# Layer 3 of a DLRM tower with samples on partitions: swapping the two operands of its matrix product

## The chip, the core and the metric

The kernel runs on one core of one Trainium2 chip. Its engines are TensorE (PE in the profile; its weight loads have a row of their own, PEld), VectorE (DVE), ScalarE (ACT), GpSimd (POOL) and SyncE (SP). Each has its own instruction stream, and they meet at semaphores. The metric is the device time of one execution in microseconds; the median of several executions counts.

## What is computed

For 2048 samples, 27 embedding tables give one row of 128 numbers each. All 351 pairs of these 27 rows are multiplied (dot products), joined with a dense feature vector of 128, and sent through three layers of 512, 256 and 1 outputs.

```python
e = jnp.stack([tbl_0[ids[:, 0]], ..., tbl_26[ids[:, 26]]], axis=1)      # 2048 x 27 x 128
interactions = jnp.einsum('bfd,bgd->bfg', e, e)                         # pairs
x = interactions.reshape(B, F * F)[:, TRIL_IDX]                         # 351 of them
z = jnp.concatenate([r_bottom_mlp_out, x], axis=1)
h = jnp.concatenate([z, r_bottom_mlp_out], axis=1)                      # 607
h = jnp.maximum(h @ W_top1 + b_top1, 0.0)                               # 512
h = jnp.maximum(h @ W_top2 + b_top2, 0.0)                               # 256
y = h @ W_top3                                                          # 1: the layer of the change
```

## The kernel before

The batch is worked in 8 half blocks of 256 samples (HALF), each of two tiles of 128 (TILE). In every half block:

- features: 11 tables of 1000 rows are read by one-hot products (onehot_unit, line 728): VectorE makes the one-hot tiles (line 433), TensorE multiplies them by the table. The other 16 tables are gathered by GpSimd (line 393) and transposed by TensorE (transpose_tile, line 740). ScalarE copies both into embT (lines 541 and 548).
- products of pairs: pair_products (line 754) for tile 0 and tile 1, in the last half block end_products (line 766). VectorE and ScalarE copy the products to SBUF (lines 446 and 559), SyncE writes them to DRAM (write_gram, line 315) and reads them back rearranged (read_pairs, line 325); ScalarE and VectorE split what was read (lines 573 and 408).
- dense layers, one half block late: while half block i has its features and products made, the layers of half block i - 1 run between them. On TensorE, second_rows(i, dense) puts them in this order: layer 1 (line 774) and layer 2 (line 802) around the transpose of tile 1's third bank, then the transpose of its fourth bank, then layer 3 (line 810), and then the products of tile 1.
- On ScalarE the order is the same: layer 2's two results (line 584), the embT copy of the fourth bank (line 548), then layer 3's copy to y (line 597), then the products' copies.
- SyncE stores y (line 295) at the end of its half; behind it stand the next ids' load (line 281) and the four gram stores of tile 1.

The order of the work is written out by hand in each engine's stream; half block 1 stands by itself, 2 to 6 are a loop (Fori) and 7 stands by itself again. In half block 7 all eight PSUM banks serve the dense layers, and its layers run alone at the end.

Layer 3 before: the weights w3 (one column for each of two chunks of 128 hidden units) are the stationary operand, and layer 2's result h2 (128 hidden units x 256 samples) streams. The result is one row of 256 on one partition. The samples of a tile stand in the order "k j" (k of 4, j of 32), where sample j * 4 + k is meant, so ScalarE's copy to y also reorders, and the store is one contiguous row of 1 KB.

Of the kernel before, what the change touches and what calls it, by code (L numbers as in the profile page):

```python
# [7 lines left out]
HALF, TILE = 256, 128  # L8
HALVES = BATCH // HALF
FIRST, LAST = 0, HALVES - 1  # L10
PAD = 32
GROUP = 4
# [10 lines left out]
def is_half(i, h):  # L23

    return isinstance(i, int) and i == h
# [31 lines left out]
def dlrm_tower(nc, bottom, ids, ids_onehot, tables, w_bottom_a, w_pairs, w_bottom_b, b1, w2, b2, w3, scratch, out):  # L57
    fp32, fp32r, i32 = mybir.dt.float32, mybir.dt.float32r, mybir.dt.int32
# [50 lines left out]
    JT = TILE // GROUP  # L109
# [9 lines left out]
    M1, M2 = H1 // 128, H2 // 128  # L119
# [20 lines left out]
    with ctx:  # L140
        def sb(name, shape, dt):
            return ctx.enter_context(nc.sbuf_tensor(name, shape, dt))
# [6 lines left out]
        KIB = 1024  # L149
# [6 lines left out]
        def in_arena(name, shape, dt, at):  # L156
            return nc.alloc_sbuf_tensor_at(name, shape, dt, offset=arena_at + at)
# [7 lines left out]
        packed = in_arena("packed", [J, GROUP, PAIRS], fp32, 13 * KIB // 2)  # L165
        pairX = in_arena("pairX", [CHUNK, 3, HALF], fp32, 13 * KIB)
        h2 = in_arena("h2", [128, M2, HALF], fp32, 16 * KIB)
        y = in_arena("y", [1, HALF], fp32, 18 * KIB)
        w1p_raw = in_weight_arena("w1p_raw", [CHUNK, 3, H1], fp32, 0)
        w1b_raw = in_weight_arena("w1b_raw", [128, H1], fp32, 6 * KIB)  # L170
        w1b_more = in_weight_arena("w1b_more", [128, H1], fp32, 12 * KIB)
# [19 lines left out]
        w3s = sb("w3s", [128, M2], fp32)  # L191
# [36 lines left out]
        dense_act = sem("dense_act")  # L228
# [4 lines left out]
        out_done = sem("out_done")  # L233
        WEIGHT_LOADS = 7
        TILE_OUT = 16 * GROUP


        def gram_piece(t, b):
# [15 lines left out]
        def dense_at(i, w):  # L254

            ring = all_banks if is_half(i, LAST) else ps_dense
            return ring[w % len(ring)]
# [12 lines left out]
        def _(sp):  # L270
# [21 lines left out]
            def store(i, at):  # L292
                sp.wait_ge(dense_act, (M2 + 1) * (i + 1))
                sp.sem_inc(loads_begun, 1)
                sp.dma_start(out[bass.ds(at, HALF), :].rearrange("b o -> o b"), y[:, :]).then_inc(out_done, 16)

            def next_ids(i, m, at, n):

# [18 lines left out]
            def read_pairs(i, some):  # L317

                if 0 in some:
                    sp.wait_ge(gram_out, TILE_OUT * 2 * (i + 1))  # L320
                    sp.sem_inc(loads_begun, 1)
# [50 lines left out]
                half(i, sp.snap(i * HALF))  # L372
            half(LAST, LAST * HALF, False)
            store(LAST, LAST * HALF)
            sp.wait_ge(out_done, 16 * HALVES)

        @block.gpsimd
        def _(pool):
# [27 lines left out]
        def _(dve):  # L406
# [30 lines left out]
            def empty_gram(i, t):  # L437
                if t == 0 and not is_half(i, FIRST):
                    dve.wait_ge(gram_out, TILE_OUT * 2 * i)
                if is_half(i, LAST):  # L440
# [71 lines left out]
        def _(act):  # L512
# [74 lines left out]
            def layer3(i):  # L587
                w = use_y(i)
                act.wait_ge(densed, DENSE * i + w + 1)
                if not is_half(i, FIRST):  # L590
                    act.wait_ge(out_done, 16 * i)
                bank = dense_at(i, w)[0:1, 0:HALF]
                if is_half(i, LAST):
                    nc.scalar.copy(y[:, :].rearrange("p (j k) -> p k j", k=GROUP),
                                   bank.rearrange("p (k j) -> p k j", k=GROUP)).then_inc(dense_act, 1)
                else:
                    nc.scalar.copy(y[:, :].rearrange("p (t j k) -> p t k j", t=2, k=GROUP),
                                   bank.rearrange("p (t k j) -> p t k j", t=2, k=GROUP)).then_inc(dense_act, 1)

            def features(i, dense=None):  # L600

# [66 lines left out]
            for u in range(1, RG, 2):  # L668
                act.wait_ge(densed, DENSE * LAST + u + 1)
                for dst, src in pack_pieces(u):  # L670
                    last = nc.scalar.copy(dst, src)
# [10 lines left out]
        def _(pe):  # L682
# [123 lines left out]
            def layer3(i):  # L806
                bank = dense_bank(i, use_y(i))
                for c in range(M2):
                    pe.wait_ge(dense_act, (M2 + 1) * i + c + 1)
                    last = nc.tensor.matmul(bank[0:1, 0:HALF], w3s[:, c:c + 1], h2[:, c, :],  # L810
                                            start=(c == 0), stop=(c == M2 - 1))
                last.then_inc(densed, 1)

            def relayout():
# [127 lines left out]
```

## Time and profile before

| | us |
|---|---|
| median of 3 runs | 408.24 |
| lowest and highest | 406.95 and 410.33 |
| span of the profiled execution | 600.9 |
| TensorE busy, matmul | 416.6 |
| TensorE busy, weight load | 378.3 |
| GpSimd busy | 253.9 |
| VectorE busy | 198.2 |
| ScalarE busy | 143.3 |

The profiled execution is a different one from the three timed ones, and its own time beside them is its span, 600.9 us. Times of rows below are microseconds from its start. A matmul with fp32 operands appears as two records, each with its own weight load. "Idle before" is the time in which the engine did nothing ahead of a group, with what ended it; "issue" means that nothing in the profile ended it. Layer 3 of the seven half blocks 0 to 6 appears once in each of seven turns, at 175.7, 246.2, 316.0, 384.9, 454.4, 524.6 and 574.9 us.

### The profile page before, as it was taken

What the parts mean: (1) busy time and instruction counts of PE and PEld (TensorE: products, weight loads), DVE (VectorE), ACT (ScalarE), POOL (GpSimd) and SP (SyncE); (2) the same over time, 40 slices, a digit from 0 to 9 for tenths busy, and PEclk for the clock granted to TensorE, in tenths of its full rate; (3) what the DMA queues carried; (4) which work ended last, traced back from release to release, by engine and by line L of the source; (5) the groups of instructions that cost most, each with busy time, mean ns of one, the idle gap of its engine ahead of it and who ended that gap; (6) DMA issues with size and microseconds to landing.
All of it is one profiled execution on the core that took longest, in us unless ns stands there. A gap on an engine that the chain in (4) does not pass through costs nothing.

```text
span 600.9 us, 11581 instructions
## 1 busy us (share of the span) xinstructions
PE 416.6 (69%) x4550; PEld 378.3 (63%) x4550; DVE 198.2 (33%) x523; ACT 143.3 (24%) x256; POOL 253.9 (42%) x263
## 2 busy tenths in 40 slices
PE   0444655786498836897298955899378972979888
PEld 0434644676388836697186944788276962979766
DVE  3405612265204612074013722065022730138111
ACT  2302321124031221224022230322122230312423
POOL 6773563256440671526622563406723365220000
PEclk9975887698597976999579985989578995889989
DMA  7964721236112461144312461124311362122000
GB/s 161 236 146 108 191 60 52 59 76 107 36 50 54 94 104 42 36 81 92 84 36 53 88 108 31 52 59 93 96 41 31 95 92 70 41 59 52 11 2 1
DMA packets 50590, 44.79 MB, mean 75 GB/s; under 512 B 30211, under 2 KB 43019, under 8 KB 50562
## 3 DMA queue, kind: packets, MB, share of 16 engines
q1 hardware_dynamic: 40746, 25.82, 22.2%
q0 software_dynamic: 8192, 16.79, 10.8%
q10 hardware_dynamic: 1623, 1.79, 1.2%
q8 instruction: 19, 0.31, 0.2%
q14 instruction: 10, 0.07, 0.0%
HBM read 39.52 MB, written 4.85 MB: 74 GB/s over the span
## 4 chain that ended last, share of the span: by engine, by line
PE 63%; issue 23%; another core or an unknown queue 5%; DVE 4%; ACT 2%; DMA 1%; SPq 1%; ACTq 0%; DVEq 0%
PE ps_build L728 26%; PE ps_gram L754 16%; PE ps_dense L774 8%; PE ps_dense L802 4%; PE ps_build L740 3%; DVE hot L433 2%; PE ps_gram L740 2%; DMA raw<-tbl_dram 1%; PE ps_dense L810 1%; PE ps_gram L774 1%; DVE table L408 1%; ACT embT L541 1%; PE ps_gram L766 1%; PE ps_gram L821 1%
## 5 line engine op out<-in xcount | busy, mean ns | idle before, releaser
L393 POOL DMA_INDIRECT rows<-tbl_dram,idx x256 | 253.1, 989 | 275.6 <-PE ps_gram L740 96.2
L728 PE MATMUL ps_build<-hot,table 125*128 125x256 f32 x1408 | 196.3, 299 | 60.1 <-DVE table L408 34.0
L728 PEld LDWEIGHTS ps_build<-hot,table 125*128 125x128 f32 x1408 | 184.9, 204 | 65.6 <-issue 53.8
L754 PE MATMUL ps_gram<-embT 128*53 128x52 f32 x1792 | 99.5, 254 | 107.2 <-issue 106.5
L754 PEld LDWEIGHTS ps_gram<-embT 128*53 128x53 f32 x1792 | 80.8, 166 | 127.9 <-issue 125.4
L433 DVE TENSOR_SCALAR hot<-id_raw 125x512 fp32r<-125x512 f32 (+1 forms) x384 | 133.8, 408 | 76.4 <-remote 33.3
L446 DVE COPY gram<-ps_gram 117x416 f32<-117x416 f32 x28 | 16.6, 592 | 229.8 <-remote 151.1
L541 ACT COPY embT<-ps_build 128x512 f32<-128x512 f32 (+1 forms) x48 | 37.7, 786 | 176.9 <-PE ps_build L728 82.8
L559 ACT COPY gram<-ps_gram 117x416 f32<-117x416 f32 x28 | 14.2, 506 | 178.7 <-PE ps_gram L754 130.1
L774 PE MATMUL ps_dense<-pairT,w1p 120*128 120x256 f32 (+1 forms) x252 | 37.1, 295 | 0.0
L774 PEld LDWEIGHTS ps_dense<-pairT,w1p 120*128 120x128 f32 (+1 forms) x252 | 34.9, 206 | 0.0
L740 PE MATMUL ps_build<-ident,rows 128*128 128x128 f32 x128 | 20.4, 286 | 8.8 <-issue 6.9
L802 PE MATMUL ps_dense<-h,w2s 128*128 128x256 f32 x112 | 25.3, 379 | 0.0
L423 DVE TENSOR_SCALAR id_raw<-id_raw,vocab 125x512 f32<-125x512 int32 (+1 forms) x48 | 22.2, 462 | 6.2 <-DMA id_raw<-ids_onehot_dram 6.2
L548 ACT COPY embT<-ps_build 128x512 f32<-128x512 f32 x32 | 21.4, 669 | 7.4 <-PE ps_build L740 4.9
L548 ACT COPY embT<-ps_gram 128x512 f32<-128x512 f32 x32 | 21.6, 675 | 4.2 <-DVE w1b L408 2.2
L740 PEld LDWEIGHTS ps_build<-ident,rows 128*128 128x128 f32 x128 | 15.4, 146 | 11.4 <-issue 10.6
L802 PEld LDWEIGHTS ps_dense<-h,w2s 128*128 128x128 f32 x112 | 20.8, 190 | 2.6
L579 ACT ACTIVATE h<-ps_dense,b1s 128x256 f32<-128x256 f32 x28 | 13.3, 473 | 30.6 <-PE ps_dense L774 30.6
L408 DVE TENSOR_TENSOR pairT<-pairX,pairT 120x256 fp32r<-120x256 f32 (+1 forms) x21 | 7.7, 421 | 36.0 <-issue 18.9
L740 PE MATMUL ps_gram<-ident,rows 128*128 128x128 f32 x128 | 19.3, 272 | 0.0
L774 PE MATMUL ps_dense<-botT,w1b 128*128 128x256 f32 x84 | 17.6, 323 | 0.0
(57 smaller groups left out, 147.6 us busy)
## 6 DMA issues: line engine op xcount, KB each, us to landing
id_raw<-ids_onehot_dram SPq DMA_DIRECT2D x40, 256.0 KB
raw<-tbl_dram SPq DMA_DIRECT2D x11, 448.0 KB
gram_dram<-gram SPq DMA_DIRECT2D x56, 84.5 KB
rows<-tbl_dram,idx POOLq DMA_INDIRECT x256
id_raw<-ids_onehot_dram SPq DMA_DIRECT2D x8, 128.0 KB
bot<-bottom_dram SPq DMA_DIRECT2D x8, 128.0 KB
w1p_raw<-w_pairs_dram ACTq DMA_DIRECT2D x1, 720.0 KB
raw<-tbl_dram SPq DMA_DIRECT2D x11, 52.0 KB
```

The lines of the kernel that those rows point to most:

```text
L393: nc.gpsimd.indirect_dma_start(rows[:, t, s * D:(s + 1) * D], None, tables[f], bass.IndirectOffsetOnAxis(idx[:, 2 * i + t, f:f + 1], 0)).t ...
L423: nc.vector.tensor_scalar(shifted, id_raw[0:VP, n % ID_SLOTS, 0:w, :], vocab[0:VP, 0:1], None, ALU.subtract).then_inc(id_shifted, 1)
L433: last = nc.vector.tensor_scalar(hot[0:VP, a % HOT_SLOTS, v, 0:w, :], shifted, float(v0 + v), None, ALU.is_equal)
L446: nc.vector.tensor_copy(*gram_piece(t, 2 * n + 0)).then_inc(gram_dve, 1)
L541: nc.scalar.copy(embT[:, :, f:f + n], src).then_inc(emb_done, 1)
L548: nc.scalar.copy(embT[:, t * TILE:(t + 1) * TILE, u * FQ:u * FQ + n], src).then_inc(emb_done, 1)
L559: nc.scalar.copy(*gram_piece(t, 2 * n + 1)).then_inc(gram_act, 1)
L728: last = nc.tensor.matmul(bank[:, q * HALF:(q + 1) * HALF], table[0:VP, units[n][q], bits, row:row + D], hot[0:VP, a % HOT_SLOTS, v, q, :] ...
L740: last = nc.tensor.transpose(bank[:, f * 128:(f + 1) * 128], rows[:, t, s * D:(s + 1) * D], ident[:, :])
L754: last = nc.tensor.matmul(gram_banks[b][STRIP * q:STRIP * q + GM - STRIP, g * DUO * PG:(g + 1) * DUO * PG], x.rearrange("p k g -> p (k g)" ...
L774: last = nc.tensor.matmul(bank, w(a), x(b), start=(first and m == 0), stop=(end and m == 2))
L802: last = nc.tensor.matmul(bank[:, 0:HALF], w2s[:, c, cols], h1[:, c, :], start=(c == 0), stop=(c == M1 - 1))
```

## The change

For half blocks 0 to 6 the operands of layer 3 change places. h2 of one tile of 128 samples becomes the stationary operand, w3's one column streams, and the result is 128 partitions (samples) x 1; two tiles give two columns, and two chunks of hidden units accumulate into each. ScalarE copies 128 x 2 to a new y of that shape. As partition k * 32 + j holds sample j * 4 + k of its tile, the reordering moves into the store: four stores, one for each k, of 32 partitions x 2 elements. The last half block keeps the row form, with a tile of its own (y_end). The counts of the semaphore out_done change with the number of stores, and layer 3 of the last half block doesn't wait on it any more.

```diff
--- before.py
+++ after.py
@@ -165,7 +165,8 @@
         packed = in_arena("packed", [J, GROUP, PAIRS], fp32, 13 * KIB // 2)
         pairX = in_arena("pairX", [CHUNK, 3, HALF], fp32, 13 * KIB)
         h2 = in_arena("h2", [128, M2, HALF], fp32, 16 * KIB)
-        y = in_arena("y", [1, HALF], fp32, 18 * KIB)
+        y = in_arena("y", [128, 2], fp32, 18 * KIB)
+        y_end = in_arena("y_end", [1, HALF], fp32, 18 * KIB + 32)
         w1p_raw = in_weight_arena("w1p_raw", [CHUNK, 3, H1], fp32, 0)
         w1b_raw = in_weight_arena("w1b_raw", [128, H1], fp32, 6 * KIB)
         w1b_more = in_weight_arena("w1b_more", [128, H1], fp32, 12 * KIB)
@@ -233,6 +234,7 @@
         out_done = sem("out_done")
         WEIGHT_LOADS = 7
         TILE_OUT = 16 * GROUP
+        HALF_OUT = 16 * GROUP
 
 
         def gram_piece(t, b):
@@ -292,7 +294,12 @@
             def store(i, at):
                 sp.wait_ge(dense_act, (M2 + 1) * (i + 1))
                 sp.sem_inc(loads_begun, 1)
-                sp.dma_start(out[bass.ds(at, HALF), :].rearrange("b o -> o b"), y[:, :]).then_inc(out_done, 16)
+                if is_half(i, LAST):
+                    sp.dma_start(out[bass.ds(at, HALF), :].rearrange("b o -> o b"), y_end[:, :]).then_inc(out_done, 16)
+                else:
+                    dst = out[bass.ds(at, HALF), :].rearrange("(t j k) o -> k j (t o)", t=2, k=GROUP)
+                    for k in range(GROUP):
+                        sp.dma_start(dst[k], y[k * JT:(k + 1) * JT, :], allow_slow_non_contiguous=True).then_inc(out_done, 16)
 
             def next_ids(i, m, at, n):
 
@@ -372,7 +379,7 @@
                 half(i, sp.snap(i * HALF))
             half(LAST, LAST * HALF, False)
             store(LAST, LAST * HALF)
-            sp.wait_ge(out_done, 16 * HALVES)
+            sp.wait_ge(out_done, HALF_OUT * LAST + 16)
 
         @block.gpsimd
         def _(pool):
@@ -587,15 +594,14 @@
             def layer3(i):
                 w = use_y(i)
                 act.wait_ge(densed, DENSE * i + w + 1)
-                if not is_half(i, FIRST):
-                    act.wait_ge(out_done, 16 * i)
-                bank = dense_at(i, w)[0:1, 0:HALF]
                 if is_half(i, LAST):
-                    nc.scalar.copy(y[:, :].rearrange("p (j k) -> p k j", k=GROUP),
+                    bank = dense_at(i, w)[0:1, 0:HALF]
+                    nc.scalar.copy(y_end[:, :].rearrange("p (j k) -> p k j", k=GROUP),
                                    bank.rearrange("p (k j) -> p k j", k=GROUP)).then_inc(dense_act, 1)
                 else:
-                    nc.scalar.copy(y[:, :].rearrange("p (t j k) -> p t k j", t=2, k=GROUP),
-                                   bank.rearrange("p (t k j) -> p t k j", t=2, k=GROUP)).then_inc(dense_act, 1)
+                    if not is_half(i, FIRST):
+                        act.wait_ge(out_done, HALF_OUT * i)
+                    nc.scalar.copy(y[:, :], dense_at(i, w)[:, 0:2]).then_inc(dense_act, 1)
 
             def features(i, dense=None):
 
@@ -807,8 +813,13 @@
                 bank = dense_bank(i, use_y(i))
                 for c in range(M2):
                     pe.wait_ge(dense_act, (M2 + 1) * i + c + 1)
-                    last = nc.tensor.matmul(bank[0:1, 0:HALF], w3s[:, c:c + 1], h2[:, c, :],
-                                            start=(c == 0), stop=(c == M2 - 1))
+                    if is_half(i, LAST):
+                        last = nc.tensor.matmul(bank[0:1, 0:HALF], w3s[:, c:c + 1], h2[:, c, :],
+                                                start=(c == 0), stop=(c == M2 - 1))
+                        continue
+                    for t in range(2):
+                        last = nc.tensor.matmul(bank[:, t:t + 1], h2[:, c, t * TILE:(t + 1) * TILE], w3s[:, c:c + 1],
+                                                start=(c == t == 0), stop=(c == M2 - 1), skip_group_check=True)
                 last.then_inc(densed, 1)
 
             def relayout():
```

## Rows read from the trace of the kernel before

**Rows 1.** The page's costliest groups: busy us, mean ns | idle before.

```profile
L754 PE MATMUL ps_gram<-embT 128*53 128x52 f32 x1792 | 99.5, 254 | 107.2 <-issue 106.5
```

**Rows 2.** The chain of waits, 380 to 395 us: start, us, what.

```profile
384.96 0.95 PE ps_dense L810 x4
385.92 1.65 PE ps_gram L754 x53
```

**Rows 3.** Windows: busy PE, PEld, DVE, ACT, POOL, clock, DMA share, GB/s.

```profile
351.70:374.00 22.30, 9.28 (x129) 6.95 (x128) 2.89 (x7) 2.21 (x6) 11.97 (x13) 0.57 0.31 64
374.00:384.90 10.90, 10.90 (x74) 10.26 (x74) 1.22 (x4) 3.85 (x8) 3.77 (x4) 0.94 0.21 56
384.90:394.00 9.10, 6.21 (x134) 4.85 (x133) 1.94 (x5) 1.88 (x4) 3.77 (x4) 0.92 0.11 29
394.00:424.00 30.00, 26.25 (x209) 25.08 (x210) 16.84 (x48) 8.19 (x13) 12.95 (x13) 0.96 0.38 84
```

**Rows 4.** Timeline around layer 3: start, us, what, [idle before].

```profile
384.36 0.60 PE L740 MATMUL ps_build<-ident,rows 128*128 128x128 f32 x4
384.56 0.47 ACT L584 ACTIVATE h<-ps_dense,b2s 128x256 f32<-128x256 f32 x1 [1.25 <-PE ps_dense L802]
...
384.89 1.02 PE L810 MATMUL ps_dense<-h,w3s 128*1 128x256 f32 x4
385.00 0.66 ACT L548 COPY embT<-ps_build 128x512 f32<-128x512 f32 x1
385.85 0.77 PEld L754 LDWEIGHTS ps_gram<-embT 128*53 128x53 f32 x28 [0.44 <-issue]
...
386.03 0.62 ACT L597 COPY y<-ps_dense 1x256 f32<-1x256 f32 x1 [0.38 <-PE ps_dense L810]
```

**Rows 5.** Line 810 over the whole run: ns min/median/max.

```profile
L810 PE MATMUL ps_dense<-h,w3s x32: 377/378/379, 175.7 to 598.3; 128*1 128x256 f32 x32
```

**Rows 6.** Timeline behind layer 3, first and last of seven turns.

```profile
176.65 1.64 PEld L754 LDWEIGHTS ps_gram<-embT 128*53 128x53 f32 x54 [0.44 <-ACT embT L548]
...
574.94 1.02 PE L810 MATMUL ps_dense<-h,w3s 128*1 128x256 f32 x4
...
575.76 1.43 PE L766 MATMUL ps_gram<-embT 128*26 128x26 f32 x146
```

**Rows 7.** Line 740 into ps_build, whole run: ns min/median/max.

```profile
L740 PE MATMUL ps_build<-ident,rows x128: 270/273/475, 79.3 to 574.7; 128*128 128x128 f32 x128
```

**Rows 8.** Timeline of TensorE, 587.24 to 587.62 us, line 832.

```profile
587.25 0.55 PE L832 MATMUL ps_dense<-ident,packed 64*111 64x64 f32 x4
```

**Rows 9.** Groups by shape, 586 to 588 us: busy, mean ns | idle.

```profile
L832 PE MATMUL ps_dense<-ident,packed 64*111 64x64 f32 x4 | 0.6, 258 | 0.0
...
L832 PE MATMUL ps_dense<-ident,packed 64*120 64x64 f32 x4 | 0.4, 219 | 0.0
```

**Rows 10.** The timelines of ScalarE and VectorE, 386 to 397 us.

```profile
391.92 0.51 ACT L559 COPY gram<-ps_gram 117x416 f32<-117x416 f32 x1 [5.27 <-PE ps_gram L754]
...
392.65 0.59 DVE L446 COPY gram<-ps_gram 117x416 f32<-117x416 f32 x1 [2.51 <-PE ps_gram L754]
```

**Rows 11.** Timeline of SyncE behind the y store.

```profile
394.83 0.41 SPq L281 DMA_DIRECT2D id_raw<-ids_onehot_dram  x1
395.47 1.56 SPq L315 DMA_DIRECT2D gram_dram<-gram  x4
```

**Rows 12.** Line 518, the load of w3: ns min/median/max.

```profile
L518 ACTq DMA_DIRECT2D w3s<-w_dram x1: 1394/1394/1394, 62.2 to 62.2; - x1
```

**Rows 13.** Timelines of SyncE and ScalarE, one turn later.

```profile
406.87 8.37 SPq L325 DMA_DIRECT2D pairX<-gram_dram  x21
...
425.59 1.01 ACT L573 CAST pairT<-pairX 120x256 fp32r<-120x256 f32 x3
```

**Rows 14.** Windows of layer 3 and of line 754 at 0.50.

```profile
384.90:385.85 0.95, 0.95 (x6) 0.25 (x5) 0.00 (x0) 0.76 (x2) 0.00 (x0) 1.00 0.01 0
370.40:374.00 3.60, 3.58 (x74) 3.49 (x74) 1.79 (x4) 0.51 (x1) 0.00 (x0) 0.50 0.00 0
```

## The prediction, made before the result

> **What bounds the kernel now.** First the page's costliest groups. The profiled execution spans 600.9 us, and before the pair products (line 754) TensorE sat idle for 106.5 us in which it waited for nothing that the profile shows [rows 1]. The unprofiled median is 408.24 us, 192.7 below the span, so much of that idle time comes with the recording. I therefore make the sum as a difference to the profiled execution (600.9 us), stage by stage, where a stage isn't stretched, and put the same difference on the median. The place of the change isn't stretched: in the chain of waits layer 3 and the first 53 products of line 754 follow each other without such a gap [rows 2].
>
> Second, the windows by stage of one turn of the loop. Layers 1 and 2 (374.0 to 384.9) keep TensorE busy for 10.90 of 10.90 us, the features (394 to 424) for 26.25 of 30, the first tile's products only 9.28 of 22.3 [rows 3]. So unprofiled, a turn is mostly TensorE's, and a microsecond that layer 3 adds to or takes from TensorE's chain would count, seven times.
>
> Third, what ends last at layer 3, in order of time [rows 4]. TensorE starts layer 3 at 384.89 and the next stage, line 754, at 385.85: 0.96 us. That stage needs the features' last copy, ScalarE's line 548, which runs from 385.00 to 385.66. Line 754 follows it by 0.19 us. The four matrix multiplications of layer 3 stand 0.214 us apart ((1.02 - 0.378) / 3, [rows 4, 5]), so they hold TensorE for 4 x 0.214 = 0.86 us, to 385.75. Both are close, but the copy is the later by a little once its 0.19 us is added: in the first of the seven turns the idle time of the weight load, 0.44 us, is put down to this copy in so many words, and in the last, where line 766 follows after 0.82 us, again [rows 6]. **Layer 3 lies beside a copy that has to happen anyway.**
>
> **The change part by part.** It concerns the seven half blocks 0 to 6; half block 7 keeps its row form.
>
> *TensorE, removed:* two multiplications of one weight column by 256 samples. Each shows as two pairs of weight load and matmul: 4 records, 0.86 us.
>
> *TensorE, added:* four multiplications (two chunks of 128 hidden units, two tiles of 128 samples), each loading 128 columns and streaming one: 8 pairs. The matmul is now nearly nothing, so the pace is that of the weight load. No row has a 128-column load with a 1-column matmul. Bound from above: the transposes of line 740 load 128 columns and stream 128 at (0.60 - 0.273) / 3 = 0.109 us a pair [rows 4, 7], 8 x 0.109 = 0.87 us. The loads of 111 columns with 64 streamed go at (0.55 - 0.258) / 3 = 0.097 us [rows 8, 9]; scaled to 128 columns 0.112, or 0.90 us. Bound from below: the four pairs with 120 columns that follow them are busy for 0.4 us at 219 ns for one, so (0.4 - 0.22) / 3 = 0.06 us a pair [rows 9], 8 x 0.06 = 0.48 us. I take 0.87, since only line 740 has the full 128 columns. Then layer 3 ends at 384.89 + 0.87 = 385.76 where it ended at 385.75. At either end of 0.48 to 0.90 line 754, at 0.96, doesn't move. In the one turn with 0.82 us it could move by 0.08 at most. The second chunk waits for line 584's second result, ready at 385.04 [rows 4]; four pairs of the first chunk last until 385.1 to 385.3, so that wait costs nothing either. Cost: 7 turns x 0 = 0, at most +0.1 us in all.
>
> The Trainium skill (TensorE: Matmul & The Clock Gate, section LDWEIGHTS) has the load take its column count divided by 1.2, 107 ns for 128, and 8 of these would be 0.85 us; the 111-column rows agree with it, the 120-column rows at 0.06 us do not. Either way the sum stays zero.
>
> *ScalarE:* the copy of one row of 256 elements (0.62 us, [rows 4]) becomes one of 128 rows of 2. It can save between nothing and all of the 0.62 us; with 2 elements a row I take most of it, 0.4. What counts is who waits for its end: after the y copy ScalarE stands idle until the products' copy at 391.92, 5.27 us [rows 10]. Even at 53 products in 1.65 us [rows 2], half of the 128 records of this tile (1792 over 14 tiles, [rows 1]) takes 2.0 us and would let it start at 385.85 + 2.0 = 387.9, 1.2 us behind the old y copy's end (386.65). Both ends are worth 0.
>
> *SyncE:* four store issues for one. Today's y store is one row of 1 KB. Each new one has 64 elements of 4 bytes, which lie 16 bytes apart in the output. From below, the four gram stores took 1.56 us to issue [rows 11]; from above, the load of w3 (128 x 2 elements, more than any of the four has) took 1394 ns, so four would take 5.6 us [rows 12]. I take 1.6, as those are SyncE's own. What is queued behind them: the ids' load and the four gram stores of the second tile, next seen at 394.83 [rows 11]. They wait for VectorE, and come 394.83 - 392.65 = 2.2 us after it begins its last products' copy [rows 10, 11]. Without the recording's gaps that copy follows three quarters of 4.0 us of products: 385.85 + 3.0 + 2.2 = 391.0. The stores begin by 386.7 and end at 388.3, or 392.3 at the upper end: 1.3 us late. That lateness is covered too: the last 21 reads behind the gram stores are issued from 406.87 to 415.24, and the first copy that needs what was read runs at 425.59, right behind another copy and with no idle time before it [rows 13]. Cost 0.
>
> The Trainium skill (DMA: Bandwidth & Descriptors, section Rules for kernel authors) speaks against the new store: a last dimension that isn't contiguous lowers to one descriptor per element. By that rule a half block makes 256 small writes in place of one. The DMA share is 0.11 in this stage [rows 3], so there is room for them beside other work.
>
> *Waits:* ScalarE's wait for the earlier stores is met a whole turn before. The last half block no longer has it, and its own store and its end are the same as before.
>
> Sum: 0 to +0.1 us. The profiled span should be near 601 us (28 more pairs to record may add a few us there and nowhere else), and the median 408.24 + 0 = 408.2 us. The three runs of before spread from 406.95 to 410.33, which is most of my width.
>
> **The rivals.**
>
> *Layer 3 does end last when nothing is recorded (faster).* If TensorE ran at its lower level (1.2 GHz) here, the old multiplications would take 4 x 0.43 = 1.72 us, past the copy, and the new ones, if the load keeps its pace, 0.90. Line 754 would come 1.72 - 0.96 = 0.76 us earlier, 7 x 0.76 = 5.3 us: 402.9 us. Against it: the granted clock is 1.00 in that stretch, and all 32 records of line 810 took 377 to 379 ns, in all eight half blocks [rows 5, 14]. At full clock with the copy out of the way, the gain would be at most (0.86 - 0.48) x 7 = 2.7 us, within 1%. Chance 0.05.
>
> *The weight loads don't hide under one column (slower).* If each load had to wait out the short matmul before it, a pair would cost the load, at most the 0.109 us of a line 740 pair, and the 219 ns of the shortest matmul in these rows [rows 7, 9]: 8 x 0.328 = 2.62 us. Line 754 would begin 2.62 - 0.96 = 1.66 us later, 7 x 1.66 = 11.6 us: 419.8 us. It decides from the point at which a pair takes over 0.96 / 8 = 0.12 us, and line 740 with 0.109 is not far below. Against it: pairs that start 0.097 us apart while one matmul lasts 258 ns can only be had if each load runs under the matmul before it [rows 8, 9]. Chance 0.06.
>
> *The clock falls behind layer 3 (slower).* One streamed column leaves the array nearly idle for 0.9 us, next to four transposes. At a granted clock of 0.50, 74 records of line 754 took 3.58 us, at 1.00 53 took 1.65 [rows 2, 14]: 0.048 against 0.031 us each. A tile of 128 would cost 2.2 us more, 7 x 2.2 = 15.4 us: 423.6 us. Against it: the clock was 0.57 where TensorE stood idle for more than half of 22.3 us, and 0.94 over layers 1 and 2 behind it [rows 3]; here no idle stretch is added, and layers 1 and 2, fully busy, lie ahead. Chance 0.03.
>
> **How the numbers follow.** Forecast 0.86 at 408.2 us, faster rival 0.05, slower ones 0.06 and 0.03. The predicted time is the forecast's. Under 1% is about what a measurement of this kernel can tell from no change, so the forecast and its bounds lie in "same". Range: the forecast's terms reach from -2.7 (the copy out of the way) to +0.1, with a run's spread of -1.3 to +2.1 around the median; I take 404.8 to 412.0, which leaves out the rivals, 0.14 together (the faster one stays 1.9 below the low end), and some of the upper end of the spread around a new median.
>
> **What would show it.** In the changed kernel's trace: eight pairs of the new layer 3 starting 0.06 to 0.11 us apart; line 754's stage still starting 0.19 us behind the end of the embT copy, with the same 0.96 us from layer 3's start; a y copy near 0.2 us; four y stores that end before the ids' load behind them is released, and pair copies on ScalarE with no idle time ahead. It would be wrong if the pairs stand more than 0.12 us apart, if the clock under line 754's second tile is lower than now in its gapless part, or if a store takes over 3 us to issue.

## The result, and the profile after

| | median us | lowest to highest | executions |
|---|---|---|---|
| before, beside the changed kernel | 407.60 | 402.54 to 410.33 | 4 |
| changed | 412.56 | 411.11 to 412.89 | 4 |

The ratio is 1.0147, with a 95% interval of 1.0103 to 1.0192. Forecast were 408.2 us and "same"; the measured time lies above the range (404.8 to 412.0), and the interval above 1%.

There are sessions in which every kernel of this study, the one before included, takes about 600 us, and others in which it takes about 410, on the same chip too. The trace on which the prediction rests is from a session of the first kind; the times it was set against, and the changed kernel's trace, are from the second. So the gap of 192.7 us wasn't the recording: the profiled execution of before_b spans 409.8 us, and the executions beside it took 410. Below, rows are compared within one kind.

The changed kernel's layer 3, in the middle of the loop (timeline, start, us, what, [idle before]); it answers to [rows 4]:

```profile
249.31 0.60 PE L746 MATMUL ps_build<-ident,rows 128*128 128x128 f32 x4
249.51 0.47 ACT L591 ACTIVATE h<-ps_dense,b2s 128x256 f32<-128x256 f32 x1 [1.25 <-PE ps_dense L808]
249.64 0.97 PEld L821 LDWEIGHTS ps_dense<-w3s,h 128*128 128x128 f32 x8
249.74 0.95 PE L821 MATMUL ps_dense<-w3s,h 128*128 128x1 f32 x8
...
249.94 0.66 ACT L555 COPY embT<-ps_build 128x512 f32<-128x512 f32 x1
...
250.73 1.28 PE L760 MATMUL ps_gram<-embT 128*53 128x52 f32 x43
250.81 0.16 ACT L604 COPY y<-ps_dense 128x2 f32<-128x2 f32 x1 [0.20 <-PE ps_dense L821]
```

The same place in the kernel before, from a later trace of it (before_b) in a session of the same kind:

```profile
252.57 0.60 PE L740 MATMUL ps_build<-ident,rows 128*128 128x128 f32 x4
...
253.10 1.02 PE L810 MATMUL ps_dense<-h,w3s 128*1 128x256 f32 x4
...
253.21 0.66 ACT L548 COPY embT<-ps_build 128x512 f32<-128x512 f32 x1
254.06 1.26 PEld L754 LDWEIGHTS ps_gram<-embT 128*53 128x53 f32 x48 [0.44 <-issue]
```

Read both from the transposes' start. The products of pairs follow after 250.73 - 249.31 = 1.42 us in the changed kernel and after 254.06 - 252.57 = 1.49 us before. Layer 3 doesn't cost TensorE anything here; it gains some hundredths of a microsecond, as its first weight load starts right behind the transposes' last one, where the one-column load came 0.17 us late. In the loop, layer 3 comes again every 42.81 to 42.86 us in the changed kernel and every 42.87 to 42.97 before (249.74 to 292.56, and 210.23 to 253.10, are two of these turns). The gain is too small to count on: in a second trace of the changed kernel (after_b) two of the turns took 43.03 and 43.04 us, with 0.2 us more idle time before the one-hot products. So the loss is not in the loop. It is at the end, behind layer 3 of half block 6.

TensorE's timeline there, changed kernel:

```profile
381.22 0.95 PE L821 MATMUL ps_dense<-w3s,h 128*128 128x1 f32 x8
382.13 1.38 PE L772 MATMUL ps_gram<-embT 128*26 128x26 f32 x142
385.74 1.18 PE L772 MATMUL ps_gram<-embT 128*26 128x26 f32 x109 [2.23 <-issue]
389.14 0.31 PE L772 MATMUL ps_gram<-embT 128*26 128x26 f32 x5 [2.21 <-issue]
390.18 1.81 PE L832 MATMUL ps_dense<-ident,gram_end 122*64 122x122 f32 x8 [0.73 <-issue]
```

and before:

```profile
384.93 1.02 PE L810 MATMUL ps_dense<-h,w3s 128*1 128x256 f32 x4
385.75 1.50 PE L766 MATMUL ps_gram<-embT 128*26 128x26 f32 x154
389.50 1.24 PE L766 MATMUL ps_gram<-embT 128*26 128x26 f32 x102 [2.25 <-issue]
391.38 1.81 PE L821 MATMUL ps_dense<-ident,gram_end 122*64 122x122 f32 x8 [0.64 <-issue]
```

There is one idle stretch of 2.2 us more that waited for nothing the profile shows, and the relayout (the transposes of the last products, line 832, before 821) begins 390.18 - 381.22 = 8.96 us behind layer 3 instead of 391.38 - 384.93 = 6.45: **2.5 us lost, once per execution.**

The profile doesn't say what TensorE waits for there, but one thing in the DMA queues has changed with it. Queue q8 carries instructions, in packets of 16 KB: 19 in both kernels, and 20 in a kernel with 232 more instructions on TensorE (after_pad232, below). A window of 3.5 us around the one that counts, changed kernel first (packets, MB, share of 16 engines):

```profile
q8 instruction: 1, 0.02, 4.9%
```

```profile
q8 instruction: 1, 0.02, 1.6%
```

A share of 4.9% of 16 engines over 3.5 us is one engine for 0.049 x 16 x 3.5 = 2.7 us; 1.6% is 0.9 us. The same 16 KB of instructions take three times as long (2.75 and 0.88 us by the packets' own records), though no other packet moves in either window: the last of the 4-byte packets of the stores starts 4.55 us behind layer 3, and the block starts at 5.59. The Trainium skill (Runtime: NRT & Kernel Launch, section Instruction fetch mechanics) says that an engine's sequencer fetches its program over a DMA queue of its own in blocks of 16 KiB, 256 instructions, and calls the cost of a boundary "mostly hidden". The blocks are as the trace has them. That they are hidden doesn't fit this stage, where a tile of line 766 is 256 pairs of load and product, two blocks: in every trace each of the two tiles has an idle stretch of 2.0 to 2.7 us in it that ends 1.2 to 1.6 us behind the landing of a block.

### The profile page after: what moved, and what is told of

Same layout as the page of the kernel before. It is cut to its first block, busy times and chain, and to the rows that moved or that the text cites. A ratio compares the mean times of both kernels' runs of the same rounds, so it can differ in the third digit from the quotient of the medians.

```text
span 409.1 us, 11687 instructions
## 1 busy us (share of the span) xinstructions
PE 356.5 (87%) x4578; PEld 343.2 (84%) x4578; DVE 202.9 (50%) x523; ACT 138.6 (34%) x256; POOL 261.6 (64%) x263
## 4 chain that ended last, share of the span: by engine, by line
PE 82%; issue 7%; ACT 5%; DVE 3%; DMA 2%; SPq 1%; ACTq 0%; DVEq 0%
PE ps_build L734 41%; PE ps_gram L760 11%; PE ps_dense L780 11%; PE ps_dense L808 6%; PE ps_build L746 3%; PE ps_gram L746 3%; ACT embT L548 3%; DMA raw<-tbl_dram 2%; PE ps_gram L780 1%; DVE hot L440 1%; PE ps_dense L821 1%; PE ps_gram L772 1%; ACT embT L555 1%; DVE table L415 1%; PE ps_build L808 1%
## 5 line engine op out<-in xcount | busy, mean ns | idle before, releaser
L400 POOL DMA_INDIRECT rows<-tbl_dram,idx x256 | 260.9, 1019 | 85.9 <-issue 73.8
L734 PE MATMUL ps_build<-hot,table 125*128 125x256 f32 x1408 | 190.8, 296 | 32.3 <-DVE table L415 19.6
L734 PEld LDWEIGHTS ps_build<-hot,table 125*128 125x128 f32 x1408 | 181.8, 202 | 35.2 <-issue 25.5
L440 DVE TENSOR_SCALAR hot<-id_raw 125x512 fp32r<-125x512 f32 (+1 forms) x384 | 139.2, 418 | 35.7 <-PE ps_build L734 31.0
L760 PE MATMUL ps_gram<-embT 128*53 128x52 f32 x1792 | 47.0, 213 | 1.0 <-ACT embT L555 0.9
L760 PEld LDWEIGHTS ps_gram<-embT 128*53 128x53 f32 x1792 | 45.2, 129 | 2.9 <-ACT embT L555 2.3
L529 ACT CAST table<-raw 125x1024 fp32r<-125x1024 f32 x11 | 11.4, 1050 | 21.0 <-DMA raw<-tbl_dram 21.0
```

Of the source, the lines that this page charges most:

```text
L400: nc.gpsimd.indirect_dma_start(rows[:, t, s * D:(s + 1) * D], None, tables[f], bass.IndirectOffsetOnAxis(idx[:, 2 * i + t, f:f + 1], 0)).t ...
L440: last = nc.vector.tensor_scalar(hot[0:VP, a % HOT_SLOTS, v, 0:w, :], shifted, float(v0 + v), None, ALU.is_equal)
L734: last = nc.tensor.matmul(bank[:, q * HALF:(q + 1) * HALF], table[0:VP, units[n][q], bits, row:row + D], hot[0:VP, a % HOT_SLOTS, v, q, :] ...
L760: last = nc.tensor.matmul(gram_banks[b][STRIP * q:STRIP * q + GM - STRIP, g * DUO * PG:(g + 1) * DUO * PG], x.rearrange("p k g -> p (k g)" ...
```

## Experiments

Comparison runs of the kernel before are shared within a session. "Layer 3 to relayout" is from the first record of layer 3 of half block 6 to the first of line 821 (832 and so on), "to the last layer 3" as far as the last layer 3's first record, both worked out from the traces' starts; one trace stands for each row; "block" is the duration of the second 16 KB packet of q8 behind that layer 3. All traces of the study:

| kernel | session | small stores at the end of half block 6 | block us | layer 3 to relayout | to the last layer 3 |
|---|---|---|---|---|---|
| before (first trace) | 600 | no | 1.09 | 6.01 | 22.73 |
| before_again | 600 | no | 1.03 | 6.27 | 21.82 |
| before_c | 600 | no | 1.24 | 6.51 | 21.52 |
| before_b | 410 | no | 0.88 | 6.45 | 21.57 |
| before_pad24 | 600 | no | 1.03 | 6.39 | 22.17 |
| swap_in_loop | 600 | no | 1.02 | 6.09 | 21.90 |
| swap_one_store | 600 | one, 8-byte rows | 1.22 | 6.76 | 22.37 |
| store_late | 410 | moved away | 0.91 | 6.35 | 26.09 |
| rows_four_stores | 600 | four | 2.73 | 8.29 | 24.39 |
| changed | 410 | four | 2.75 | 8.96 | 24.66 |
| after_b (changed) | 410 | four | 2.71 | 8.88 | 24.43 |
| after_again (changed) | 600 | four | 2.32 | 8.38 | 24.29 |
| after_pad232 | 600 | four | 2.87 | 8.63 | 24.86 |
| swap_sorted | 410 | one, 256 x 4 bytes | 2.78 | 10.97 | 27.66 |

**Is it the product or the stores?** The theories at the start: P, the swapped product costs TensorE time; S, the four stores cost it; N, neither does, and the difference is one of executions.

> The kernel before, unchanged, for a profile that isn't stretched and as a check of the comparison. Theory P (the swapped product on TensorE costs the time), theory S (the four stores cost it) and theory N (the changed kernel costs nothing in a turn; the 1.5% come from somewhere that varies between executions) all expect a ratio of 1.00 here. They differ in its profile: under P and S a turn of the loop is shorter than the 42.83 us of the changed kernel, by about 5 us / 7 = 0.7 us; under N it is 42.8 us as well, or 42.9, since layer 3's place was 1.16 us from the last transpose in the old profile and is 1.10 us in the changed kernel's.

> The changed kernel, unchanged, on the same chip as the others. P and S: ratio 1.010 to 1.019 as measured before. N: below 1.008.

The store alone taken back (swap_one_store, which leaves out the samples' order):

```diff
-                    dst = out[bass.ds(at, HALF), :].rearrange("(t j k) o -> k j (t o)", t=2, k=GROUP)
-                    for k in range(GROUP):
-                        sp.dma_start(dst[k], y[k * JT:(k + 1) * JT, :], ...).then_inc(out_done, 16)
+                    dst = out[bass.ds(at, HALF), :].rearrange("(p t) o -> p (t o)", t=2)
+                    sp.dma_start(dst, y[:, :]).then_inc(out_done, 16)
```

> The swapped product alone: one store of 128 rows of 8 bytes in place of four of 32 x 2 elements, so the samples of a half block lie in the output in another order. P: ratio near 1.015, as the changed kernel. S: 1.00 to 1.003. N: as the changed kernel beside it, below 1.008.

The stores alone, on the kernel before (rows_four_stores):

```diff
-                sp.dma_start(out[bass.ds(at, HALF), :].rearrange("b o -> o b"), y[:, :]).then_inc(out_done, 16)
+                dst = out[bass.ds(at, HALF), :].rearrange("(n k) o -> k o n", k=GROUP)
+                src = y[:, :].rearrange("p (n k) -> p k n", k=GROUP)
+                for k in range(GROUP):
+                    sp.dma_start(dst[k], src[:, k, :], ...).then_inc(out_done, 16)
```

(all half blocks but the last)

> The old product with four stores of 64 separate elements of 4 bytes each in place of one of 1 KB. P: ratio 1.00. S: near 1.015. N: 1.00.

This was a session of 600 us. Medians: before 605.94 (11 executions, 592.82 to 611.74), the same kernel again 605.20, changed 606.36, swap_one_store 603.47, rows_four_stores 606.28. No two can be told apart; intervals were up to 2.2% wide, and even before_again alone spread over 589 to 612. Set against the three lowest of the executions of before, the others come out 1.2% to 1.9% longer (after_again 1.018, swap_one_store 1.012, rows_four_stores 1.019), but these three are picked out of a spread of 19 us, and in the later session before_pad24, whose layer 3 and store are those of before, comes out at 1.013 in the same way. By time, this batch decides nothing. Its traces say more, in the table: the row form with four stores has the long block and the late relayout, the swapped product with one store of 8-byte rows has neither. TensorE's timeline of rows_four_stores, whose layer 3 is the old one:

```profile
573.46 1.02 PE L817 MATMUL ps_dense<-h,w3s 128*1 128x256 f32 x4
574.29 1.50 PE L773 MATMUL ps_gram<-embT 128*26 128x26 f32 x154
577.76 1.16 PE L773 MATMUL ps_gram<-embT 128*26 128x26 f32 x102 [1.97 <-issue]
581.75 1.81 PE L828 MATMUL ps_dense<-ident,gram_end 122*64 122x122 f32 x8 [2.83 <-issue]
```

Here the lost time falls just behind the products, 2.83 us idle in place of 0.64. The relayout needs ScalarE's copy of the last products, and that copy waits for them: it starts at 581.15, 2.2 us behind the end of the last product's record (578.92), where it comes 0.03 us behind in before_b (390.77 and 390.74).

```profile
581.15 0.51 ACT L562 COPY gram_end<-ps_gram 122x416 f32<-122x416 f32 x1 [5.95 <-remote]
```

**How much do executions differ?** Both kernels once more, many times.

> The kernel before, once more. In the four runs ahead of this one every kernel took 589 to 617 us, and the differences between them drowned in that spread, so this one looks for a session in which it takes 408 us as in the first times. If it does: theory P or S expects a turn of the loop of 42.1 us in its trace, 0.7 us under the changed kernel's 42.83; theory N expects 42.8 to 42.9 us, and the difference of 5 us in what lies outside the turns or in TensorE's clock.

> The changed kernel, many times. In the last run the kernel before spread from 403.6 to 417.3 us over 29 executions, each with its granted clock (0.942 to 0.979), and its turn of the loop took 42.87 us against 42.83 in the changed kernel's trace. Theory N: the four executions of the changed kernel (411.1 to 412.9 us at 0.954 to 0.958) were the slower part of the same spread; its median over 12 lies within 0.5% of the kernel before beside it, it has executions under 408 us too, and at an equal granted clock the two take the same within 1 us. Theory P or S, a cost in every execution: median 1.0% to 1.9% above, and 4 to 6 us more at an equal clock. Theory F: the changed program has 8 more instructions of TensorE in every half block, and a stall of TensorE's instruction stream (2.2 us, once more in the changed kernel's last half block than in the other trace) comes with that: 2 to 3 us more at an equal clock, median 0.5 to 0.8% above.

Both sessions were of the 410 us kind. before_b: 411.27 us against 409.96 for the same kernel beside it, ratio 1.0003 (0.9928 to 1.0079). after_b: 409.79 against 409.22, ratio 1.0028 (0.9976 to 1.0080). With a later session there are 51 executions of the kernel before, median 409.96 us, from 402.54 to 417.26, and 10 of the changed one, median 411.47 us, 406.60 to 413.44. The time goes with the mean granted clock of the execution: a line through 47 of before has 3.3 us less for 0.01 more clock, and scatters by 1.3 us around it. At 0.954 it took 411.3 and 412.0, at 0.966 from 407.0 to 409.2, at 0.979 it took 403.6 and 404.8. Against that line the changed kernel's ten lie 0.8 us higher in the mean, with a standard error of 0.4 from their own scatter alone; if the stores also lower the clock, the line hides that part.

So N was largely right about the first comparison: its four executions of before (median 407.6) look like a low draw from a population around 410.0, its four of the changed kernel like a high one. Of the 5.0 us, the pooled medians leave 411.47 - 409.96 = 1.5, and the comparison of after_b (0.9976 to 1.0080) doesn't tell the change's cost from zero. But N expected nothing at all in the changed kernel, and both its traces of this kind have about 2.5 us at the end (8.96 and 8.88 against 6.45). P fell: it needed turns 0.7 us longer than those of before, and they are 42.81 to 43.04 against 42.87 to 42.97 us.

**What delays the relayout: the block's edge, or the stores?** Theory F held that 24 more instructions of TensorE ahead of the last products (8 in each of the three places where layer 3 is written out) move an edge of a block into them: the first run of line 766 is 142 records long, before it was 154, 12 pairs or 24 instructions less.

> The kernel before, for a second profile beside the three below. Theory F (the program of TensorE is loaded in blocks of 16 KB, and 24 more instructions ahead of the last half block's products move a block's edge into them) expects the last stretch, from layer 3 of half block 6 to the end, at 24.9 us again, with stalls after 154 records of line 766 and none after the 102 behind them. Theory N (no difference but the clock's phase) expects this stretch anywhere between 24.9 and 27.9 us.

```diff
             pe.wait_ge(consts_made, 3)
+            for _ in range(6):
+                nc.tensor.matmul(ps_dense[1][0:1, 0:1], ident[:, 0:1], ident[:, 0:1], start=True, stop=True)
```

(before_pad24; in after_pad232 it is `range(58)`, on the changed kernel)

> The kernel before with layer 3 and its store untouched, and 24 more instructions of TensorE at its very start (6 small products of one column by one, into a bank not yet used), where TensorE waits for 16 us anyway. F: the third stall of 2.2 us appears in line 766's second tile, near 142, 109 and 5 records, and the last stretch is 27.5 to 28 us; the loop's turn stays 42.87 us. P, S and N: 24.9 us, no third stall.

> The changed kernel with 232 more instructions at the same place (58 small products), so that with its own 24 the blocks' edges lie 256 instructions on, one block of 16 KB, and meet the last half block as before. F: no third stall, last stretch near 24.9 us; the turn stays 42.83 us. P, S and N: 27.8 us as in the changed kernel's two traces.

In swap_in_loop, layer 3 and its store have the new form only where the half block is the loop's register:

```diff
+        def in_row(i):
+
+            return isinstance(i, int)
...
-                    if is_half(i, LAST):
+                    if in_row(i):
                         last = nc.tensor.matmul(bank[0:1, 0:HALF], w3s[:, c:c + 1], h2[:, c, :], ...)
```

> The change in half blocks 1 to 5 alone, those of the loop; 0 and 6 keep the row form with their one store. TensorE then has 8 instructions more ahead of the last products instead of 24. F: the turn is 42.83 us, the edge moves by 4 records (150 and 106 or more), so no third stall: last stretch 24.9 us, and in all 0.2 us less than before. P and S: nearly the full cost, since five of seven turns have it: 3 to 4 us above before.

The session was of the 600 us kind again: medians 601.49 (before_c), 595.37, 604.17 and 596.12 against 592.36 for before, which itself went from 584.5 to 606.4; nothing follows from them. The traces settle F. (before_c repeats the kernel before: idle after 154 records of line 766, and 24.8 us from layer 3 of half block 6 to the end.) TensorE's timeline of before_pad24:

```profile
570.41 1.40 PE L766 MATMUL ps_gram<-embT 128*26 128x26 f32 x142
574.17 1.15 PE L766 MATMUL ps_gram<-embT 128*26 128x26 f32 x114 [2.36 <-issue]
575.98 1.81 PE L821 MATMUL ps_dense<-ident,gram_end 122*64 122x122 f32 x8 [0.66 <-issue]
```

The edge moved to 142 as F had it, and the third stall didn't come. With after_pad232 it moved back to 154, and the relayout was late all the same, at 8.63 us. **F is wrong:** where the lost time is there, the edge only goes with whether it appears ahead of the last few products or behind them. swap_in_loop, with 5 of 7 half blocks changed but the old store at half block 6, has the early relayout (6.09 us). What all late ones share is the small stores of half block 6. Theory S', as reworded: these stores hold up the block of instructions whose fetch starts 1 to 2 us after the last of them is issued. Two kernels for it:

```diff
-                store(i - 1, at - HALF)
+                if not is_half(i, LAST):
+                    store(i - 1, at - HALF)
...
+            sp.wait_ge(h1_made, M1 * LAST + 1)
+            store(LAST - 1, (LAST - 1) * HALF)
             store(LAST, LAST * HALF)
```

> The changed kernel with the four stores of half block 6 moved from behind its layer 3 to the end, when half block 7's first layer 1 result is there. Reading behind it: in the five traces with four stores at half block 6's end (changed kernel three times, the one with 232 more instructions, the row form with four stores) the second block of TensorE's instructions behind it (queue q8, 16 KB, 5.4 to 6.1 us after layer 3's start) took 2.3 to 2.9 us to load, and from layer 3 of half block 6 to the last layer 3 it was 24.3 to 24.9 us; in the seven without, 0.9 to 1.2 us and 21.5 to 22.7 us. Theory S' (these stores hold that load up) expects 0.9 to 1.4 us for the block and 21.5 to 22.7 us here, so 2.4 us less than the changed kernel. Theory F (where the block's edges fall) expects it to stay at 24.3 or more, since TensorE's program is the changed kernel's, instruction for instruction.

TensorE's timeline of store_late:

```profile
386.12 0.95 PE L824 MATMUL ps_dense<-w3s,h 128*128 128x1 f32 x8
387.03 1.39 PE L775 MATMUL ps_gram<-embT 128*26 128x26 f32 x142
390.65 1.15 PE L775 MATMUL ps_gram<-embT 128*26 128x26 f32 x114 [2.24 <-issue]
392.46 1.81 PE L835 MATMUL ps_dense<-ident,gram_end 122*64 122x122 f32 x8 [0.66 <-issue]
```

With the changed kernel's own program on TensorE, the block takes 0.91 us, there is no third stall, and the relayout begins at 6.35 us. **So the stores make the relayout late.** That they do it through the block is not shown. Here the products end at 391.80, and the block's packet only starts at 391.87, so the products didn't need it; in the changed kernel TensorE goes on at 389.14, 0.4 us before the long packet ends (386.80 + 2.75 = 389.55), where it went on 1.2 to 1.6 us behind the packet after each of the other stalls. The long packet and the late relayout come together in all six traces that have either; what holds TensorE up stays open. The second number that S' gave, 21.5 to 22.7 us to the last layer 3, was missed: 26.09. The windows say where (us, busy of PE, PEld, DVE, ACT, POOL, clock, DMA share, GB/s), store_late first, then before_b for the same two stages, the relayout and what follows it:

```profile
392.40:398.40 6.00, 5.47 (x26) 4.39 (x26) 2.40 (x15) 1.82 (x13) 0.00 (x0) 0.50 0.00 0
398.40:412.20 13.80, 13.54 (x76) 12.67 (x77) 1.27 (x3) 3.62 (x9) 0.00 (x0) 0.75 0.02 1
```

```profile
391.20:395.80 4.60, 3.85 (x26) 3.35 (x27) 2.38 (x15) 1.94 (x14) 0.00 (x0) 0.76 0.00 0
395.80:406.50 10.70, 10.45 (x76) 9.67 (x77) 1.15 (x3) 3.54 (x9) 0.00 (x0) 1.00 0.01 2
```

TensorE's clock stayed at its lower level for longer in this execution, at the same work: 4.5 us. The moved stores can't be what did it. They are issued from 405.69 us on, and store_late's clock was low before that and at its higher level behind it:

```profile
400.23:405.69 5.46, 5.46 (x27) 5.46 (x27) 0.85 (x2) 0.90 (x3) 0.00 (x0) 0.52 0.00 0
405.69:408.36 2.67, 2.67 (x24) 2.67 (x23) 0.00 (x0) 0.95 (x2) 0.00 (x0) 1.00 0.06 0
```

Layer 2, which runs behind them, took 3.85 us against 3.84 in before_b. What kept the clock low in this execution is open; executions differ in their mean clock, as said above. The times are 410.76 us (408.86 to 417.54, 4) against 410.84 for before, ratio 1.0035 (0.9951 to 1.0119): no difference.

The last kernel keeps the small writes and takes the number of stores away. ScalarE writes layer 2's result in sorted order, so one store does:

```diff
-                nc.scalar.activation(h2[:, m, :], dense_at(i, w)[:, 0:HALF], ACT.Relu,
+                dst, src = h2[:, m, :], dense_at(i, w)[:, 0:HALF]
+                if not is_half(i, LAST):
+                    dst = dst.rearrange("p (t j k) -> p t k j", t=2, k=GROUP)
+                    src = src.rearrange("p (t k j) -> p t k j", t=2, k=GROUP)
+                nc.scalar.activation(dst, src, ACT.Relu,
...
+                    dst = out[bass.ds(at, HALF), :].rearrange("(t p) o -> p (t o)", t=2)
+                    sp.dma_start(dst, y[:, :], ...).then_inc(out_done, 16)
```

> The swapped product with one store: ScalarE writes layer 2's result with the samples sorted, so that partition p holds sample p of its tile, and one store writes 128 rows of 2 separate elements, 256 writes of 4 bytes as before. It tells the number of stores from the number of small writes. If S' is a matter of the writes (256 of 4 bytes on their way to memory), the block takes 2.3 to 2.9 us again and the stretch is 24.3 to 24.9 us. If it is a matter of four issues, the last of which begins 3.4 us after layer 3, the block takes 0.9 to 1.4 us and the stretch is 21.5 to 22.7 us. The turn of the loop stays at 42.83 us where TensorE isn't held up otherwise.

The block took 2.78 us and the relayout began at 10.97: it is the writes and not the number of issues. But the expectation that the turn stays at 42.83 us was badly off. This kernel takes 441.39 us (436.98 to 451.57), 1.076 of before (1.066 to 1.087), and from one layer 3 to the next it takes 44.8 to 57.4 us. Its edit also makes ScalarE's two results of layer 2 longer, 0.72 us each in place of 0.47, but that is 0.5 us a turn. In the loop's turns of over 50 us, TensorE stands idle among the one-hot products about 10.5 us behind layer 3, for nothing that the profile shows (TensorE's timeline of swap_sorted):

```profile
227.08 0.37 PE L737 MATMUL ps_build<-hot,table 125*128 125x256 f32 x1 [3.81 <-issue]
```

No 16 KB packet moves between 170 and 380 us of this trace. So TensorE is held up where no block of its program is on the way, which is a second reason to leave open that the block is what it waits for at half block 6. Windows of 7 us that begin 2.5 us behind a turn's layer 3, for before_b, the changed kernel and swap_sorted:

```profile
255.60:262.60 7.00, 7.00 (x118) 6.94 (x115) 4.12 (x12) 2.08 (x4) 5.41 (x6) 1.00 0.25 64
```

```profile
252.20:259.20 7.00, 7.00 (x121) 6.94 (x116) 4.20 (x11) 2.07 (x4) 5.29 (x6) 1.00 0.77 47
```

```profile
270.00:277.00 7.00, 7.00 (x122) 6.94 (x119) 4.16 (x11) 1.99 (x4) 5.33 (x6) 1.00 1.03 35
```

The packets' times add up to 25%, 77% and 103% of what 16 engines have, and they move 64, 47 and 35 GB/s. The small packets themselves are short in the records, 9 ns. What is long is what comes behind them. Here are the gathers' queue in about 4 us of the same stretches, before_b and the changed kernel:

```profile
q0 software_dynamic: 96, 0.20, 20.9%
```

```profile
q0 software_dynamic: 71, 0.16, 81.5%
```

Worked out from the packets, the 4 KB packets of a gather that start 2.5 to 7 us behind layer 3 took 264 ns in the mean before, 1312 in the changed kernel and 1819 with the sorted store, and up to 1.1, 4.9 and 7.3 us. In the loop the changed kernel's gathers have room for that: its turns aren't longer. At half block 6 there are no gathers left; what is seen behind the writes there is a block of TensorE's instructions, and TensorE is late.

**A version that beats both.** swap_in_loop has the early relayout, and would gain 0.05 us a turn if every turn were like those of the changed kernel's first trace. It ran in a session of 600 us (596.12 against 592.36, with executions of before between 584.5 and 606.4), and 0.3 us in all is far below what can be told here. None was found that is measurably faster than the kernel before.

## Why the prediction was wrong

- *Layer 3 beside the embT copy, no cost to TensorE:* right. Pairs start 0.11 us apart ((0.95 - 0.17) / 7, line 821), near the upper bound of 0.112 from the 111-column loads, not the 0.06 of the 120-column ones. The products follow the copy's end (250.60) by 0.13 us. A turn is no longer than before, but for 0.2 us in two turns of after_b.
- *The y copy:* forecast near 0.2 us, measured 0.16; worth nothing, right.
- *SyncE's queue:* four issues take 2.02 us in the loop where I took 1.6, and end at 253.2, with the next issue at 255.75. Covered, right. In the last half block one issue took 1.3 us by itself.
- *"There is room for them beside other work", the stores at cost 0:* **this step failed.** I judged the 256 small writes by the DMA share of the stage in a middle turn (0.11, [rows 3]), as though a write took engine time in proportion to its bytes. The runs show that packets that start behind it take longer: a gather's 1.3 us in the mean in place of 0.26, the block 2.3 to 2.9 us in place of 0.9 to 1.2. And I looked for what is behind in one turn of the loop only, where it is gathers with slack. At half block 6 the last products or their completion come late behind the writes, and the relayout begins 8.3 to 9.0 us behind layer 3 with the four stores instead of 6.0 to 6.8: about 2.5 us once, 0.6%. Moved away (store_late), it begins at 6.35. By what way the writes hold TensorE up stays open. None of the signs of being wrong that I had named came.
- *The rule on stores* was named and then priced at nothing. The Trainium skill (DMA: Bandwidth & Descriptors, section Rules for kernel authors) has one descriptor per element for a last dimension that isn't contiguous. The trace agrees: behind layer 3 of half block 6 there are 320 packets of 4 bytes, 256 for the elements and 16 more for each of the four stores.
- *"Much of that idle time comes with the recording":* wrong. Whole sessions run at 600 us. The idle time before line 754 [rows 1] is there in each of their traces (106.6 us in before_again) and is 1.2 us in before_b. What makes those sessions longer is open; every kernel is hit alike.
- *The range:* half its width came from a spread of three executions, 406.95 to 410.33. Over 51 it is 402.5 to 417.3, and the median 410.0 instead of 408.2. With the shift of 1.5 to 2.5 us that the pooled medians and the traces give, 411.5 to 412.5 would have been the centre. So of the first comparison's 5.0 us, about half at most is the writes and the rest is the draw of the executions. That it came out above the range was in part luck (the median of after_b, 409.79 us, lies inside it); the failed step rests on the traces and not on it.
- *The rivals:* none happened in these traces. Weight loads do hide under one column. The clock was 1.00 in the loop, as before. From layer 3 of half block 6 to the last layer 3 it was 0.86 against 0.92 (windows 381.2 to 405.9 and 384.9 to 406.5); the first holds the third idle stretch of 2.2 us and the second doesn't, so I put the lower clock down to the stall, and not to layer 3. No run separates the two.

## What to carry to other kernels

A store of single 4-byte elements is not priced by its bytes or its issue, but by what happens in the microseconds behind it; look at the places where the usual cover is missing, above all the last turn, and look at the queue of an engine's own program too. When a result has to be turned, turn it on an engine, so that the store stays one row, as the kernel before does. And before a range is drawn from three executions of a kernel whose TensorE clock varies, ask what 0.01 of mean clock is worth: here 3.3 us, more than the change.

## What was not expected of the hardware

- 256 writes of 4 bytes cost more in one store than in four. In the four, a store's neighbours in memory are 16 bytes apart; in the one (swap_sorted), neighbours touch. The time went from 411 to 441 us, of which ScalarE's longer results can explain 0.5 us a turn; why the rest is so much is open. One store of 128 rows of 8 bytes left the instruction block at 1.22 us and the relayout at 6.76.
- TensorE's program comes in 16 KB packets, 19 per execution. In the changed kernel none comes between 167.6 and 347.3 us, while the loop repeats. In code that is run for the first time there is idle time that nothing in the profile ends: 2.0 to 2.7 us in each tile of each trace's last products, ending 1.2 to 1.6 us behind a block's landing, and 5.0 and 6.3 us in half block 1 of the changed kernel and of before_b, where a block starts 2.3 and 2.5 us before its end.
- Weight loads of 128 columns with one streamed column start 0.11 us apart at a granted clock of 1.00.
